# One queue order over all rounds for attention and routed experts, with every pad row scattered instead of pre-filled

## The chip, the cores and the metric

One of the cores of one Trainium2 chip runs the kernel. The metric is the device time of one execution in microseconds (us): median, lowest and highest of the runs. Next to it stands one profiled execution, from which every row below is taken.

## What is computed

The input is 16 sequences of 512 tokens with 256 features. Each token is normalised, and attention and a mixture of experts (MoE), both fed by the normalised token, are added to it:

```python
xn = layernorm(x)
x = x + attn(xn) + moe(xn)

# attention, per sequence: 16 heads, 16 wide for q and k, 64 wide for v and the gates
q, k, v = l2norm(q), l2norm(k), l2norm(v)
sim  = einsum('bhid,bhjd->bhij', q, k)
aggr = einsum('bhij,bhjd->bhid', square(relu(sim)), v)
attn = (tanh(|aggr|) * aggr/|aggr| * tanh(silu(gates))) @ Wout

# MoE: 16 experts of width 128, 4 for each token, from the 2 best of 4 groups, and 2 shared experts
scores = sigmoid(xn @ router.T)
tidx, tw = top4 of the experts in the best two groups; tw = 2.5 * tw / sum(tw)
moe = sum_k tw[k] * down_e(silu(gate_e(xn)) * up_e(xn)) + shared(xn)
```

## The kernel before

**Set-up.** For two sequences at a time SP (the queue that only issues DMAs) loads tokens into `xs`, DVE normalises them (`layernorm`), TensorE turns them, ACT writes the high fp16 half of the turned tokens and POOL the low one (both in `xhl`), and SP stores rows (`xn_d`) and turned tokens (`xt_d`) to HBM. `xhl` has two buffers, so ACT waits for a store to land before it writes again. ACT and DVE also split the weights into two fp16 halves (`high_parts`, `low_parts`). After each pair of sequences SP issues one `fill_slots`: it writes copies of a pad row over an eighth of `slot_d`, the table of 144 blocks of 256 token rows, by expert, through which the routed experts get their tokens. Then `route()` on DVE works out for each token and choice its slot (`slot_no`) and weight (`slot_w`), and the expert of each block (`blk_w`).

**Sixteen rounds**, one sequence each, follow. A round has four stages:

- *head*: the value projections (`V`, 8 of them), the q/k norms on DVE, their fp16 split on ACT and POOL (`split_lo_qk`, 8 operations on POOL), the turns `T` into `qt` and `kt`
- *S*: 32 steps; each has two score products `S` on TensorE, a relu on ACT, a square on DVE and four value products `AV` (two steps behind)
- *tail*: head norms and their chain of small DVE operations, the turn `WT` of the scales
- *O*: 8 output products `O`; each waits for `a_lo`, a subtraction on POOL. The gates `G`, `WB` and the next round's `QK` stand between them. Then DVE takes the two results out (`finish`), and POOL adds them to the output with an accumulating DMA, here called the base add. Its count is `base_added`.

The shared experts take four units in each round, each an up part (`SG`), a high part on ACT and a low part on POOL (`HH`, `hidden_lo`), and a down part (`SD`).

**Rounds 0 to 3** also send the token rows: `send_rows` (`RW`, 16 in each round, in S at every second step) waits for a row tile from SP, copies weight and token number beside the rows, and issues four indirect DMAs to `slot_d`. There are two tile buffers (`xrow`).

**Rounds 4 to 15** also compute 12 blocks each, all inside S. A block is a chain of six items, one step apart: `XT` (turn, TensorE; the high half on ACT), `XL` (low half, DVE), `GU` (gate and up on TensorE, silu on ACT, product on DVE), `HR` (high part on ACT, low part on POOL), `DN` (down on TensorE, `block_out` on DVE), `SC` (`send_block`: POOL issues two indirect DMAs that add 256 rows to the output; it waits for the previous block's rows to have landed).

Every engine executes its own list in order, and the lists are written out by hand: `plan_steps` says at which step an item stands, `tail` what follows the last step, `pe_order` TensorE's list. Three PSUM banks `wk` go round in the order of that list (`RING`), and an operation that fills one waits until its use three places earlier has been emptied.

## Time and profile before

| | |
|---|---|
| median of 3 runs | 3089.48 us (3085.49 to 3090.55) |
| the profiled execution | 3091.26 us, of which the span is 3089.5 us |
| busy shares of the span | TensorE 73%, DVE 59%, ACT 50%, POOL 46% |
| granted TensorE clock, mean | 0.931 |

How to read the rows of the next sections: a row of stretches gives the stretch, its length, then busy us and count of instructions of PE (TensorE), PEld (its weight loads), DVE, ACT and POOL, the granted clock as a share of full speed, the DMA engines' busy share and GB/s. A row of waits says which engine and line waited for which, us in total, times, and the longest. A row of the chain that ended last has start, us, and what ran (a name that begins with DMA is a transfer landing). A row of the order of time has start, us, engine, line, operation, and in brackets idle time before it and what ended it. A grouped row has busy us and mean ns, then the idle time before the group.

### The profile page before, as it was taken

What the parts mean: (1) busy time and instruction counts of PE and PEld (TensorE: products, weight loads), DVE (VectorE), ACT (ScalarE), POOL (GpSimd) and SP (SyncE); (2) the same over time, 40 slices, a digit from 0 to 9 for tenths busy, and PEclk for the clock granted to TensorE, in tenths of its full rate; (3) what the DMA queues carried; (4) which work ended last, traced back from release to release, by engine and by line L of the source; (5) the groups of instructions that cost most, each with busy time, mean ns of one, the idle gap of its engine ahead of it and who ended that gap; (6) DMA issues with size and microseconds to landing.
All of it is one profiled execution on the core that took longest, in us unless ns stands there. A gap on an engine that the chain in (4) does not pass through costs nothing.

```text
span 3089.5 us, 41253 instructions
## 1 busy us (share of the span) xinstructions
PE 2243.1 (73%) x13476; PEld 1210.7 (39%) x13476; DVE 1831.9 (59%) x2961; ACT 1535.4 (50%) x2396; POOL 1423.7 (46%) x1339
## 2 busy tenths in 40 slices
PE   4433758484838887877878787878788787878877
PEld 3322233232314444444434444444444444444443
DVE  6678537272726555565656556565656656565654
ACT  2313536262625555555555555554555455555554
POOL 1211747566663534444353544435354444435343
PEclk9999979697978999999999999999999999999999
DMA  9992433333341413223141322213032222314132
GB/s 354 327 338 95 146 88 117 110 94 118 89 154 18 66 28 49 46 34 53 26 64 21 57 40 37 47 32 64 15 62 35 45 45 31 59 19 66 21 50 40
DMA packets 161519, 247.27 MB, mean 80 GB/s; under 512 B 14945, under 2 KB 147041, under 8 KB 159361
## 3 DMA queue, kind: packets, MB, share of 16 engines
q1 hardware_dynamic: 99104, 164.63, 17.0%
q0 software_dynamic: 62208, 79.99, 15.8%
q8 instruction: 117, 1.92, 0.2%
q14 instruction: 90, 0.73, 0.1%
HBM read 147.84 MB, written 144.25 MB: 95 GB/s over the span
## 4 chain that ended last, share of the span: by engine, by line
PE 37%; issue 21%; POOL 12%; DVE 12%; DMA 11%; ACT 5%; SPq 0%; ACTq 0%; DVEq 0%; POOLq 0%
PE wk L1175 14%; PE av L1259 7%; POOL slot_d L1101 6%; PE acc L1175 6%; DMA out_t<-ye,xg 3%; DMA xt_d<-xhl 2%; PE sim L1244 2%; DMA xrow<-xn_d 2%; PE wk L1306 2%; PE wk L1226 2%; POOL out_t L1083 2%; ACT ring L941 2%; DMA xg<-slot_d 2%; DMA slot_d<-xrow,slot_no 2%; POOL hle L1074 2%
## 5 line engine op out<-in xcount | busy, mean ns | idle before, releaser
L656 DVE TENSOR_TENSOR pr<-ring 128x1024 f32<-128x1024 f32 x512 | 627.6, 1227 | 448.5 <-ACT ring L941 438.2
L941 ACT ACTIVATE ring<-sim 128x1024 f32<-128x1024 f32 x512 | 524.0, 1023 | 291.4 <-PE sim L1244 269.4
L1259 PE MATMUL av<-pr,v 128*64 128x512 f32 x2048 | 550.8, 618 | 20.6 <-ACT wide L975 19.2
L1083 POOL DMA_INDIRECT out_t<-ye,xg x288 | 466.1, 1618 | 69.1 <-issue 69.1
L1074 POOL TENSOR_TENSOR hle<-hfe,hhe 128x256 f16<-128x256 f32 x208 | 244.4, 1176 | 438.6 <-ACT hhe L952 434.0
L1101 POOL DMA_INDIRECT slot_d<-xrow,slot_no x256 | 294.8, 1152 | 76.3 <-issue 59.0
L706 DVE TENSOR_TENSOR gate_sb<-gate_sb,wk 128x512 f32<-128x512 f32 x128 | 87.7, 686 | 345.9 <-PE wk L1334 345.9
L1130 POOL TENSOR_TENSOR pr<-wide,pr 128x512 f16<-128x512 f32 x128 | 162.4, 1273 | 269.2 <-ACT pr L987 269.2
L1069 POOL TENSOR_TENSOR gate_sb<-ring,gate_sb 128x512 f16<-128x512 f32 x128 | 164.1, 1306 | 243.4 <-ACT gate_sb L927 243.4
L947 ACT ACTIVATE sge<-wk,inv_m 128x256 f32<-128x256 f32 x208 | 99.0, 476 | 290.4 <-PE wk L1175 290.4
L1175 PE MATMUL wk<-wa_h,xhl 128*128 128x512 f16 x768 | 199.1, 382 | 57.2 <-DVE blk_w L596 44.4
L663 DVE SCALAR_TENSOR_TENSOR hfe<-wk,up_scale,sge 128x256 f32<-128x256 f32 x208 | 100.3, 482 | 231.9 <-ACT sge L947 223.0
L1244 PE MATMUL sim<-qt,kt 64*128 64x512 f16 x1024 | 205.1, 397 | 36.2 <-issue 18.6
L1244 PEld LDWEIGHTS sim<-qt,kt 64*128 64x128 f16 x1024 | 49.7, 93 | 434.6 <-ACT ring L941 228.9
L1089 POOL TENSOR_TENSOR mark<-pair_sel 1x1 f32<-1x1 f32 x160 | 29.3, 183 | 387.9 <-DVE ye L676 324.3
L1175 PE MATMUL wk<-down_h,hhe 128*128 x288 | 80.4, 279 | 169.1 <-issue 168.6
L1175 PE MATMUL acc<-wo_h,pr 128*128 128x256 f16 x1024 | 177.0, 275 | 30.5 <-POOL pr L1130 30.5
L885 ACT ACTIVATE sq<-wk 128x512 f32<-128x512 f32 x192 | 114.4, 596 | 149.2 <-PE wk L1175 149.2
L1175 PE MATMUL acc<-down_h,hhe 128*128 128x256 f16 x128 | 41.8, 326 | 198.2 <-POOL hle L1074 198.2
L1226 PE MATMUL wk<-id,gate_sb 128*128 128x128 f16 x1024 | 90.9, 265 | 102.8 <-DVE hfe L663 102.8
L1175 PE MATMUL wk<-xhl,wa_h 128*128 128x512 f16 x512 | 162.6, 401 | 2.4 <-ACT gate_sb L980 2.4
L980 ACT ACTIVATE gate_sb<-wk,inv_a 128x512 f32<-128x512 f32 x128 | 87.7, 685 | 153.6 <-PE wk L1175 153.6
(222 smaller groups left out, 4643.4 us busy)
## 6 DMA issues: line engine op xcount, KB each, us to landing
xg<-slot_d SPq DMA_DIRECT2D x147, 258.0 KB
slot_d<-pad_rows SPq DMA_DIRECT2D x8, 4644.0 KB, 19.3
xrow<-xn_d SPq DMA_DIRECT2D x64, 512.0 KB
xs<-x SPq DMA_DIRECT2D x16, 512.0 KB, 5.1
xn_d<-xs SPq DMA_DIRECT2D x16, 512.0 KB, 19.0
xt_d<-xhl SPq DMA_DIRECT2D x16, 512.0 KB, 16.5
xhl<-xt_d SPq DMA_DIRECT2D x16, 512.0 KB, 3.4
out_t<-pr POOLq DMA_DIRECT2D x16, 512.0 KB, 5.9
```

The lines of the kernel that those rows point to most:

```text
L656: tt(pr[:, n:n + 2, :], ring[:, q:q + 2, :], ring[:, q:q + 2, :], ALU.mult).then_inc(square_done, 1)
L885: a(sq[:, n % 2, :], bank(r, key)[:, :], ACT.Square).then_inc(rawsq_done, 1)
L941: a(ring[:, q:q + 2, :], sim[:, :, :], ACT.Relu).then_inc(relu_done, 1)
L1069: tt(lo, src, hi, ALU.subtract).then_inc(qk_lo, 1)
L1074: tt(hle[:, i % 2, :], hfe[:, i % 2, :], hhe[:, i % 2, :], ALU.subtract).then_inc(h_lo, 1)
L1083: pool.indirect_dma_start(out=out, out_offset=bass.IndirectOffsetOnAxis(xg[:, n % XG, j, D + 1:D + 2].bitcast(U32), 0), in_=ye[:, n % 2, j ...
L1101: pool.indirect_dma_start(out=slot_d, out_offset=bass.IndirectOffsetOnAxis(slot_no[:, k, c:c + 1], 0), in_=xrow[:, k % 2, c, :], in_offset ...
L1130: tt(al[:, t % 2, :], agg[:, t, :], ah[:, t % 2, :], ALU.subtract).then_inc(a_lo, 1)
L1175: ins = mm(dst, w[k], xx[k], start=start and i == 0, stop=stop and i == n - 1, skip_group_check=not (start and stop))
L1226: ins = turn(bank16(r, ("T", n))[:, m * P:(m + 1) * P], src[:, m * P:(m + 1) * P], id16[:, :])
L1244: ins = mm(sim[:, half, :], kt[rows, pair, j * P:(j + 1) * P], qt[rows, pair, :], start=True, stop=True)
L1259: ins = mm(av[64 * half:64 * half + 64, :], v32[:, j, h * DV:(h + 1) * DV], pr[:, (2 * s + half) % NH_, :], start=(j == 0), stop=(j == NB ...
```

## The change

The two hand-made lists per kind of round become one plan over all 16 rounds. `TICKS` cuts a round into 59 places with assumed lengths (8 `h`, 4 `t`, 32 `s`, 6 `e`, 9 `o`; 141.8 us in sum). Sixteen chains, 12 blocks and 4 shared units, start at equal distances over the round, head, tail and O included, and a chain may run over into the next round. Row tiles (`RW`) and pad tiles (`PD`) are spread over all places of rounds 0 to 3. Within a place the items stand in the order XL, SC, DN/SD, HR/HH, GU/SG, XT; those of the last place, `('o', 8)`, stand behind `finish` on DVE and behind the base add on POOL. `slot_d` is no longer filled: `route()` works out the numbers of the 4096 slots without a token (`pad_no`), and 32 indirect DMAs on POOL put pad rows there. Weight and token number come to `xrow` by a second DMA from `slot_m` and no longer by two POOL copies. `xg` has five buffers in place of three, the `mark` operations ahead of DMAs are gone, six small loads are reordered, and DVE takes `gated(t + 1)` a place earlier.

```diff
-XG = 3
+XG = 5
+EXP0 = 4
+BLOCKS = [0] * EXP0 + [12] * 12
+TICKS = ([(("h", n), 1.9) for n in range(2 * NB)] + [(("t", n), 2.6) for n in range(NB)]
+         + [(("s", n), 2.3) for n in range(STEPS)] + [(("e", n), 2.6) for n in range(6)]
+         + [(("o", n), 3.0) for n in range(NP_ + 1)])
+UP_CHAIN = (("XT", 0.0), ("XL", 2.0), ("GU", 4.2), ("HR", 7.5), ("DN", 11.0), ("SC", 13.0))
+SHARED_CHAIN = (("SG", 4.2), ("HH", 7.5), ("SD", 11.0))
...
+def plan_round_starts(b):
+    blocks = BLOCKS[b]
+    n = max(blocks + SH, 16)
+    at = [m * n // 16 for m in (1, 4, 7, 10)]
+    length = ROUND_TIME if b < B - 1 else ROUND_TIME - 14.0
...
+    for m in range(n):
+        when = b * ROUND_TIME + 0.5 + m * length / n
...
+    units = [("RW", k) for k in range(TILES)]
+    for k in range(PAD_TILES):
+        units.insert(3 * k + 2, ("PD", k))
+    places = [(b, tick) for b in range(EXP0) for tick, _ in TICKS if b < EXP0 - 1 or tick[0] != "o"]
+    for n, unit in enumerate(units):
+        plan[places[n * len(places) // len(units)]].append(unit)
...
-            def fill_slots(g):
-                n = NBLK * BLK // (B // LNG)
-                sp.dma_start(slot_d[g * n:(g + 1) * n, :].rearrange("(a r) c -> a (r c)", a=16),
-                             pad_rows.rearrange("r c -> (r c)").unsqueeze(0).to_broadcast(
-                                 [16, PADS * ROW])).then_inc(slots_set, 16)
...
+                    sp.dma_start(xrow[:, tau % 2, :, D:D + 2], slot_m[:, tau, :, :]).then_inc(rows_loaded[tau % 2], 16)
...
             def body(r):
-                for k in range(NB):
-                    split_lo_qk(r, k)
-                item(r, ("HH", 0))
-                item(r, ("HH", 1))
+                for n in range(4):
+                    items(r, "h", n)
+                split_lo_qk(r, 0)
+                items(r, "h", 4)
+                split_lo_qk(r, 1)
+                for n in range(5, 8):
+                    items(r, "h", n)
+                split_lo_qk(r, 2)
+                items(r, "t", 0)
+                split_lo_qk(r, 3)
...
                 for t in range(NP_):
                     pool.wait_ge(a_hi, r.n(NP_, t + 1))
                     pool.wait_ge(out_mm, r.n(NP_, t - 1))
                     tt(al[:, t % 2, :], agg[:, t, :], ah[:, t % 2, :], ALU.subtract).then_inc(a_lo, 1)
+                    items(r, "o", t)
                 pool.wait_ge(y_done, r.n(2, 2))
...
+                bases[0] += 1
+                items(r, "o", NP_)
```

`send_block` in its new form, on POOL; `bases[0]` counts the base adds issued so far:

```python
def send_block(g):
    pool.wait_ge(ye_done, g + 1)
    pool.wait_ge(sent, 32 * g)
    pool.wait_ge(base_added, 16 * bases[0])
    for j in range(HALVES):
        pool.indirect_dma_start(...)     # 128 rows each, added to out
```

## Rows read from the trace of the kernel before

**Rows 1.** Stretches of the set-up: to the end of the tokens, and `route()`.

```profile
66.40:191.00 124.60, 60.32 (x266) 55.27 (x265) 77.84 (x201) 41.06 (x52) 27.31 (x14) 1.00 0.97 337
191.00:269.80 78.80, 1.89 (x4) 0.43 (x4) 76.23 (x138) 0.00 (x0) 0.18 (x1) 1.00 0.75 251
```

**Rows 2.** Waits in the first 205 us.

```profile
ACT xhl L866 <- DMA xt_d<-xhl: 27.2, 9, 6.9
...
DVE stats L482 <- DMA xs<-x: 9.1, 2, 6.6
```

**Rows 3.** Stretches of round 2: head, S, tail, O.

```profile
614.40:644.40 30.00, 21.39 (x148) 13.01 (x147) 25.80 (x52) 19.99 (x37) 12.70 (x12) 0.88 0.13 18
644.40:697.90 53.50, 49.71 (x240) 16.19 (x241) 40.30 (x40) 38.77 (x45) 44.84 (x46) 0.97 0.39 129
697.90:758.80 60.90, 16.92 (x95) 8.91 (x95) 10.52 (x28) 10.04 (x18) 39.95 (x55) 0.66 0.45 147
758.80:781.70 22.90, 22.89 (x142) 13.72 (x143) 10.45 (x15) 11.92 (x20) 8.44 (x7) 0.93 0.21 70
```

**Rows 4.** Waits of round 2.

```profile
PE acc L1175 <- POOL hle L1074: 42.0, 1, 42.0
```

**Rows 5.** Stretches of round 7: head, S, tail, O.

```profile
1484.70:1514.70 30.00, 21.40 (x148) 12.97 (x147) 25.80 (x52) 20.03 (x37) 12.71 (x12) 0.88 0.13 18
1514.70:1618.30 103.60, 82.11 (x496) 41.18 (x494) 60.08 (x75) 54.89 (x82) 52.37 (x46) 0.97 0.35 54
1618.30:1640.70 22.40, 17.83 (x101) 9.10 (x101) 10.76 (x28) 9.03 (x18) 6.39 (x8) 0.92 0.20 36
1640.70:1662.00 21.30, 21.25 (x142) 13.38 (x143) 10.49 (x15) 11.96 (x20) 8.48 (x7) 1.00 0.08 26
```

**Rows 6.** The page's DMA issues: KB each, us from issue to landing.

```profile
slot_d<-pad_rows SPq DMA_DIRECT2D x8, 4644.0 KB, 19.3
...
out_t<-pr POOLq DMA_DIRECT2D x16, 512.0 KB, 5.9
out_t<-ye,xg POOLq DMA_INDIRECT x288, 3.8
```

**Rows 7.** POOL's row sends in round 0, grouped: beside S, then after it.

```profile
L1101 POOL DMA_INDIRECT slot_d<-xrow,slot_no x30 | 40.5, 1349 | 9.0 <-issue 6.7 <-POOL xrow L1097 2.3
...
L1101 POOL DMA_INDIRECT slot_d<-xrow,slot_no x35 | 34.4, 982 | 10.4 <-issue 8.5 <-POOL xrow L1097 1.9
```

**Rows 8.** The chain that ended last, tail of round 2.

```profile
719.26 3.10 DMA slot_d<-xrow,slot_no
722.38 4.19 DMA xrow<-xn_d
```

**Rows 9.** The chain that ended last, S of round 7: GU, XT, DN.

```profile
1562.44 1.50 PE wk L1175 x12
...
1564.08 0.63 PE wk L1306 x4
...
1592.79 0.82 PE wk L1175 x6
```

**Rows 10.** TensorE's down products in round 7, grouped.

```profile
L1175 PE MATMUL wk<-down_h,hhe 128*128 x24 | 6.6, 276 | 14.1 <-issue 14.0
```

**Rows 11.** POOL in order of time, S of round 7: HR, then one SC.

```profile
1567.49 1.40 POOL L1074 TENSOR_TENSOR hle<-hfe,hhe 128x256 f16<-128x256 f32 x1 [1.57 <-ACT hhe L952]
...
1571.77 1.57 POOL L1083 DMA_INDIRECT out_t<-ye,xg  x1 [0.17 <-issue]
1573.64 1.54 POOL L1083 DMA_INDIRECT out_t<-ye,xg  x1 [0.31 <-issue]
```

**Rows 12.** POOL in order of time, from round 3 to round 4.

```profile
953.14 1.30 POOL L1135 DMA_DIRECT2D out_t<-pr  x1
961.95 5.72 POOL L1069 TENSOR_TENSOR gate_sb<-ring,gate_sb 128x512 f16<-128x512 f32 x4 [7.50 <-ACT gate_sb L927]
```

**Rows 13.** The base adds by line: ns min/median/max, first and last start.

```profile
L1135 POOL DMA_DIRECT2D out_t<-pr x16: 1275/1283/1375, 446.3 to 3082.2; - x16
```

More of the change, by code:

```diff
@@ L82, in tail @@
-def tail(late):
-    return ([("AV", STEPS - 2), ("G", 0), ("SG", 2), ("N", NP_ - 2), ("AV", STEPS - 1)] + late
-            + [("HH", 2), ("SG", 3), ("N", NP_ - 1), ("G", 1), ("HH", 3), ("SD", 2), ("TH", 0), ("SD", 3),
-               ("WT", 0), ("G", 2), ("WB", 0), ("WB", 1)])
-PLAN, LATE, TAIL = {}, {}, {}
-for _kind in "AB":
-    PLAN[_kind], LATE[_kind] = plan_steps(_kind)
-    TAIL[_kind] = tail(LATE[_kind])
-def pe_order(kind):
+EXP0 = 4
+BLOCKS = [0] * EXP0 + [12] * 12
+assert len(BLOCKS) == B and sum(BLOCKS) == NBLK
@@ new lines @@
+TICKS = ([(("h", n), 1.9) for n in range(2 * NB)] + [(("t", n), 2.6) for n in range(NB)]
+         + [(("s", n), 2.3) for n in range(STEPS)] + [(("e", n), 2.6) for n in range(6)]
+         + [(("o", n), 3.0) for n in range(NP_ + 1)])
+ROUND_TIME = sum(d for _, d in TICKS)
+UP_CHAIN = (("XT", 0.0), ("XL", 2.0), ("GU", 4.2), ("HR", 7.5), ("DN", 11.0), ("SC", 13.0))
[3 more added lines that the diff above has]
+    n = max(blocks + SH, 16)
+    first = sum(BLOCKS[:b])
+    at = [m * n // 16 for m in (1, 4, 7, 10)]
+    length = ROUND_TIME if b < B - 1 else ROUND_TIME - 14.0
+    chains, g, q = [], first, 0
+    for m in range(n):
+        when = b * ROUND_TIME + 0.5 + m * length / n
+        if m in at:
+            chains.append((when, "shared", (b, q)))
+            q += 1
+        elif blocks:
+            chains.append((when, "block", g))
+            g += 1
+    assert q == SH and g == first + blocks
+    return chains
@@ new lines, in tick_at, with plan_all @@
+def tick_at(when):
+    b = min(int(when // ROUND_TIME), B - 1)
+    left = when - b * ROUND_TIME
+    for n, (_, length) in enumerate(TICKS):
+        if left < length:
+            return b * len(TICKS) + n
+        left -= length
+    return B * len(TICKS) - 1
+def plan_all():
+    plan = {(b, tick): [] for b in range(B) for tick, _ in TICKS}
+    for b in range(B):
+        for when, what, key in plan_round_starts(b):
+            n = -1
+            for kind, later in (UP_CHAIN if what == "block" else SHARED_CHAIN):
+                n = min(max(tick_at(when + later), n + 1), B * len(TICKS) - 1)
+                plan[(n // len(TICKS), TICKS[n % len(TICKS)][0])].append((kind, key))
+    stage = {"XL": 0, "SC": 1, "DN": 2, "SD": 2, "HR": 3, "HH": 3, "GU": 4, "SG": 4, "XT": 5}
+    for items in plan.values():
+        items.sort(key=lambda item: stage[item[0]])
+    units = [("RW", k) for k in range(TILES)]
[4 more added lines that the diff above has]
+        plan[places[n * len(places) // len(units)]].append(unit)
+    for b in range(B):
+        for t in range(NP_ - 2):
+            plan[(b, ("s", NB * (t + 1) + LAG + 1))].append(("N", (b, t)))
+    return plan
@@ L407, in _ @@
             sp.wait_ge(route_done, 1)
+            for n in range(2):
+                sp.dma_start(pad_row[:, n, :], pad_rows[n * P:(n + 1) * P, :]).then_inc(pads_loaded, 16)
             tau = 0
@@ L821, in body @@
                     norms_round(link_v, "v")
-                item(r, ("SG", 1))
+                items(r, "t", 1)
                 turned_q(r, 2)
@@ L1052, in body @@
                         raw(r, t - (NP_ - 2), ahead=1)
+                    items(r, "o", t)
+                items(r, "o", NP_)
             loops(act, body)
```

595 lines of the change are left out of this document (296 added, 299 removed).

## The prediction

> **What bounds the kernel now.** I read the stretches by stage first. In the set-up the DMA engines are 0.97 busy up to 191 us while DVE works 77.8 of 124.6 us; then `route()` is a pure DVE chain, 76.2 of 78.8 us [rows 1]. Part of DVE's idle time traces back to DMA: ACT waits 27.2 us in nine goes for stores of `xt_d`, DVE 9.1 us for tokens [rows 2].
>
> In a round without blocks the tail is the odd stage: 60.9 us, in which TensorE works 16.9 and POOL 40.0 [rows 3]. The waits say why: a shared down part waits once for 42.0 us for its low half on POOL [rows 4], since 16 row sends stand ahead of it in POOL's queue. In a round with blocks the tail is 22.4 us, and S, where all 12 blocks are, takes 103.6 us with TensorE busy 82.1; O is TensorE from end to end, 21.25 of 21.3 us [rows 5]. The round takes 177.3 us. The base adds give the frame [rows 12, 13]: set-up to 269.8 us, four rounds to 953.1 (683.3), twelve rounds to 3082.2 (2129.1, 177.4 each), 7.3 to the end of the span, and 1.8 outside it: 3091.3, against a median of 3089.5.
>
> **Set-up: fills out, pad numbers in.** Eight fills of 4644 KB, 38 MB, leave the queue [rows 6]. That is much of what the DMA engines carry up to 191 us, but DVE needs its busy time anyhow, and some of its waits are for ACT and POOL. I give back the 9.1 us of token waits to two thirds (6) and of ACT's 27.2 us for stores about 19, since ACT is ahead of DVE's weight pieces and of the last scores: 25 us off; bounds 10 and 36.3 (all of both rows). `route()` gets six small operations and a copy, the largest half as wide as those that fill its 76.2 us; about 3 us. Set-up: 269.8 - 25 + 3 = 248.
>
> **Rounds 0 to 3: row sends spread.** A send was four issues at 1.35 us beside S and 0.98 after it [rows 7]; with the gaps of 0.3 us between issues (9.0 us over 30) that is 6.3 and 4.8 us; the two POOL copies ahead of it go. I counted the new places from the plan: 8 sends stand in S, the others in head, tail and O, with 8 pads of one issue in each round. POOL's work per round: 8 x 6.3 + 8 x 4.8 + 8 x 1.4 = 100 us, and with the splits, `hidden_lo` and `a_lo` (12.7 + 0.9 + 8.4 busy in [rows 3] beside the sends) 122. The row tiles have two buffers: load 4.2, four issues, landing 3.1 [rows 8] make some 12.5 us for two, so 6.3 each, 100 in a round: not the bound when spread. A round without the stall is 30 + 53.5 + 22.4 (the tail of [rows 5]) + 21.3 = 127.2. POOL is close to full in that, and its sends now stand ahead of things that others wait for: about one send (5) ahead of the splits in the head, the third shared unit late by what POOL's 8 sends, pads and low parts exceed S (60 against 53.5, so 5 of it on the path), one to two sends ahead of `a_lo` at the end of the tail (7), and 3 in O. That gives 35 + 58.5 + 29.4 + 24.3 = 147.2; bounds 127 and 165 (all of the surplus late, as now). Four of them and the 7.3 us by which the first head is longer: 596, for 683.3.
>
> The small DMA for weight and token number goes out beside each tile: 512 pieces of 8 bytes. No row has such a transfer. Below, it is hidden beside the tile (the tile's 4.2 us is also 512 pieces); above, it comes after it in the same time, 8.4 in place of 4.2, and a tile takes 8.4 us in place of 6.3. I take 6.5, nearer to hidden. The Trainium skill (DMA: Bandwidth & Descriptors, Specifications) says that below 512 B the engines do a read-modify-write and lose the line rate, which speaks for the upper figure; by it the sum would be some 40 us longer, as the fourth rival works out from rows.
>
> **Rounds 4 to 15: S.** A steady round now starts 6 blocks in S, 2 in head, 1 in tail, 3 in O, and in S three shared up parts. A block is 1.50 + 0.63 + 0.82 = 2.95 us of TensorE [rows 9] (2.6 where products follow one another). S loses six blocks, 6 x 2.8 = 16.8, and gains 4.5: 82.1 - 16.8 + 4.5 = 69.8 us busy. Idle there was 21.5, of which 14 stood ahead of the down products [rows 10], as `DN` came one step after `HR` with POOL's 1.4 us and an `SC` between [rows 11]. Now it is mostly two steps. So S takes 75 (bounds 70, no idle, and 81, the old idle per block): 28.6 us less.
>
> **O and tail.** O was TensorE all through, so three blocks add 3 x 2.7 = 8. `DN` of `('o', 7)` with its result on DVE now stands ahead of the q/k sums and `finish`: +3. `SC` on POOL, 3.4 us [rows 11], stands ahead of an `a_lo` twice, about 1 us each: 34. The tail's shared units are replaced by about as much of blocks: 22.5.
>
> **Head: the new wait.** `items(r, "o", NP_)` follows the base add on POOL, and in it is the `SC` of the round's eleventh block, which waits for that base add to land. From the base add's issue: 1.3 us issue and 5.9 landing [rows 6, 12], so it goes at 7.2 and ends at 10.6. Behind it stands `HR` of the twelfth, 12.0, and TensorE, which would be at `('h', 1)` after about 3 us, waits there for that low half. The next `SC` (`h2`) must wait until the former has landed, 10.6 + 3.8 = 14.4, and ends at 17.8. Only then comes split 0, which before started at 8.8 [rows 12]: 9.0 later. Among the splits stand one more `SC` and `HR`, of which I count 3 on the path. The head is thus 30 + 12 = 42. The granted clock is 0.88 over the head now [rows 5], so 7.2 of its 30 us are at the lower of the two levels (1.2 GHz), after the engine has waited for the turns' input; that is up to 3.6 us of work. A second wait of 8 us can bring as much again; between 0 and 3.6 I take 1.5: 43.5. Round 4 has no such predecessors: 33 for its head, with two blocks in it.
>
> Round: 43.5 + 75 + 22.5 + 34 = 175, for 177.4. Round 4: 165. The last one has more in S and tail but no next `QK`: 173. Together 165 + 10 x 175 + 173 = 2088, for 2129.1.
>
> **Sum.** 248 + 596 + 2088 + 7.3 + 1.8 = 2941 us. 0.2% is 6 us, about what a measurement here can tell from no change.
>
> **Rivals.**
>
> *The base add's wait costs little* (30%). For it: TensorE has 8.6 us idle in the head [rows 5], which the new wait may only move, if the splits are not what the turns wait for. Then the head is 33, S may reach its floor of 70, and a round 33 + 72 + 22.5 + 32 = 159.5: eleven rounds by 15 less, 2941 - 165 = 2776. Against it: POOL's list is in order, and the wait is explicit.
>
> *Row sends still stall rounds 0 to 3* (12%). For it: POOL would be busy 122 of 147 us, and one late low half stops TensorE. Each round at its upper bound, 165: 4 x 18 = 72 more, 3013.
>
> *Every POOL item of head, tail and O lies on the path, and the kernel gets slower* (7%). Six `SC` and six `HR` a round leave S or sit beside it: 6 x 3.4 + 6 x 1.4 = 29 us; I have counted some 14 of it. With the other 15 a round is 190, and the whole 2941 + 165 = 3106. It decides from a round of 188.7 on: 150 us below the old time are to be used up, 13.7 in each of eleven rounds above 175.
>
> *The 8-byte pieces double the tile's load* (6%). A tile then takes 8.4 us, 16 of them 134, in a round with uneven places some 157: 4 x 10 = 40 more, 2981. The rule named above is what would make it so.
>
> My forecast has 45%. Faster: 45 + 30 + 12 + 6 = 93, of which I put 2 at no change, since the second and fourth rival together leave only some 38 us: faster 91%, same 2%, slower 7%. The forecast's own range is 2880 to 3010; with the first rival below and half of the others above it is 2770 to 3060.
>
> **What would show it.** Right: no `slot_d<-pad_rows` from SP, `route()` starting near 166; no 40 us wait on `hle` in rounds 0 to 3 and those at 140 to 155; S near 75 with six blocks; in each head from round 5 a TensorE wait of 7 to 9 us on POOL's `hle` ahead of a down product, POOL idle some 6 us after the base add's issue, and the first split at 17 to 18 us after it instead of 8.8. Wrong: a head of 33 (first rival), a tail or O far above 22 and 34 (third), POOL waiting for `xrow` over several us a tile (fourth), or a set-up still near 270, which would mean that DVE and not the DMA queue set it.

## The result, and the profile after

The changed kernel takes 3059.31 us (median of 4, 3050.23 to 3073.25), the kernel before beside it 3088.39 us (median of 4, 3085.49 to 3090.55). The ratio is 0.9911, 95% interval 0.9892 to 0.9931: 0.9% or 29 us faster. The forecast was 2941 us, 150 faster. The sign is right and the size is a fifth of what was forecast. The time lies outside the forecast's own range (2880 to 3010) and under 1 us inside the wide one (2770 to 3060). The executions that were profiled took 3073.25 and, before, 3091.3 us. The first is the longest of its four, 14 us above their median, so the stages below add up to 132 us over the forecast where the medians differ by 118. Of the four executions of `e9_e5_e8` below, one took 3853.03 us at a granted clock of 0.58; its ratio is that of the other three (2924.74 to 2933.24 us), and the 2929.45 in its table is the median of all four.

Cut into stages as in the prediction (the head from `finish` of the round before to the first relu, S from the start of the first relu to that of the last, the tail to the first output product, O to the end of `finish`), in us, mean over the rounds:

| stage | before | forecast | after |
|---|---|---|---|
| set-up with `route()` | 270.0 | 248 | 263.8 |
| rounds 0 to 3, sum | 682.9 | 596 | 605.0 |
| a round of 5 to 14: head | 29.2 | 43.5 | 42.7 |
| S | 103.4 | 75 | 81.9 |
| tail | 22.8 | 22.5 | 23.8 |
| O | 22.0 | 34 | 34.4 |
| that round | 177.4 | 175 | 182.9 |
| rounds 4 to 15, sum | 2129.1 | 2088 | 2194.0 |

So 84 us were gained up to round 3, and 65 given back in the twelve rounds after. The stretches of a round in the trace after (length, then busy time and instructions of TensorE, its weight loads, VectorE, ScalarE, GpSimd; the granted clock, the DMA engines' busy share, GB/s): head, S, tail and O of round 11.

```profile
2148.00:2190.80 42.80, 28.13 (x186) 17.57 (x183) 27.60 (x52) 22.52 (x42) 22.55 (x18) 0.84 0.35 62
2190.80:2273.00 82.20, 68.78 (x397) 30.38 (x397) 53.17 (x64) 48.58 (x69) 31.95 (x21) 0.98 0.23 36
2273.00:2297.20 24.20, 17.94 (x98) 9.09 (x95) 12.07 (x30) 9.68 (x19) 6.38 (x6) 0.86 0.19 34
2297.20:2331.60 34.40, 30.31 (x212) 20.06 (x213) 15.65 (x23) 14.40 (x27) 15.89 (x13) 1.00 0.20 32
```

Against [rows 5]: TensorE's busy time in S fell from 82.11 to 68.78 us, as forecast (69.8). But S holds 13.4 us in which it stands, where 5.2 was forecast. The granted clock in S is no lower. TensorE's two largest waits in S, round 7 before and round 11 after:

```profile
PE wk L1175 <- issue: 12.7, 10, 1.6
PE wk L1175 <- DVE xel L670: 5.1, 5, 1.6
```

```profile
PE wk L1232 <- DVE xel L705: 7.7, 5, 4.0
PE wk L1232 <- issue: 2.4, 3, 0.9
```

"issue" here is mostly a down product that waits for its low half: 12.7 us became 2.4. The wait for `xel`, the fp16 tail of a block's tokens that VectorE makes, rose. In the head TensorE stands for 14.7 us, before 8.6, at a granted clock of 0.84, before 0.88.

The set-up and round 2 (head, S, tail, O), in the same columns:

```profile
66.40:181.80 115.40, 59.90 (x264) 54.95 (x263) 75.83 (x201) 41.95 (x52) 24.20 (x13) 1.00 0.41 138
181.80:263.80 82.00, 1.89 (x4) 0.43 (x4) 79.23 (x146) 0.00 (x0) 0.00 (x0) 1.00 0.38 125
576.70:608.30 31.60, 20.51 (x138) 11.71 (x135) 26.58 (x47) 19.31 (x35) 26.31 (x24) 0.87 0.45 115
608.30:677.30 69.00, 56.74 (x276) 19.69 (x278) 41.89 (x45) 40.94 (x51) 48.87 (x43) 0.89 0.52 154
677.30:697.50 20.20, 15.49 (x65) 6.05 (x65) 8.99 (x25) 8.55 (x15) 13.39 (x13) 0.78 0.42 125
697.50:728.20 30.70, 27.06 (x145) 15.63 (x146) 13.87 (x16) 12.01 (x21) 17.08 (x16) 0.81 0.30 91
```

Against [rows 1] the DMA engines' share in the set-up fell from 0.97 to 0.41, and the stretch shortened by 9 us only; VectorE is at work for 75.8 us of it, 77.8 before. Against [rows 3] the tail fell from 60.9 to 20.2 us, and S grew by 15.5.

The head of round 11 on GpSimd, in order of time (start, length, what; in brackets the idle time ahead and what ended it), up to the second send and then the first split:

```profile
2148.28 1.36 POOL L1191 DMA_DIRECT2D out_t<-pr  x1 [5.79 <-DVE pr L752]
2154.95 1.65 POOL L1136 DMA_INDIRECT out_t<-ye,xg  x1 [5.30 <-DMA out_t<-pr]
2156.89 1.57 POOL L1136 DMA_INDIRECT out_t<-ye,xg  x1 [0.30 <-issue]
2157.90 1.27 POOL L1129 TENSOR_TENSOR hle<-hfe,hhe 128x256 f16<-128x256 f32 x1
...
2161.90 1.77 POOL L1136 DMA_INDIRECT out_t<-ye,xg  x1 [2.72 <-DVE ye L711]
...
2167.69 2.36 POOL L1124 TENSOR_TENSOR gate_sb<-ring,gate_sb 128x512 f16<-128x512 f32 x2 [2.15 <-ACT gate_sb L977]
```

and TensorE's waits of over 2 us in the same head:

```profile
2159.38 0.39 PE L1232 MATMUL wk<-down_h,hhe 128*128 x1 [6.04 <-issue]
...
2180.31 0.37 PE L1232 MATMUL acc<-down_h,hhe 128*128 128x256 f16 x1 [3.17 <-issue]
...
2186.23 1.10 PE L1283 MATMUL wk<-id,gate_sb 128*128 128x128 f16 x16 [2.16 <-DVE xel L705]
```

The wait for the base add is there as the prediction told it: the send goes 6.7 us after the add's issue (forecast 7.2), the low half 9.6 (10.6), the first split 19.4 (17 to 18). The down product waits 6.0 us for it (7 to 9).

TensorE's waits from 1000 to 2800 us, some ten rounds, grouped (us in total, times, longest), before and after:

```profile
PE wk L1175 <- issue: 143.4, 115, 1.7
PE wk L1226 <- DVE hfe L663: 63.7, 10, 6.4
PE wk L1175 <- DVE xel L670: 53.3, 51, 2.3
```

```profile
PE wk L1232 <- issue: 100.7, 49, 6.7
PE wk L1232 <- DVE xel L705: 76.2, 54, 4.0
```

The 14 us a round of "issue" became 10, of which 7.5 stand in the head (round 11), 6.0 of them behind the base add. The waits for `xel` rose from 5.3 to 7.6 us a round, though half of the blocks had left S. In S of round 11 one is of 4.0 us, at the first up product, and four are of 0.8 to 1.0: the steps with the other four up products take 3.6 to 3.9 us, where 2.3 to 2.9 are common. The prediction has no word on it. And the wait of 6.4 us in each head for `hfe` is gone, which the prediction doesn't mention either.

### The profile page after: what moved, and what is told of

The parts are those of the page before. It is cut to its first block, busy times and chain, and to the rows that moved or that the text cites. A ratio compares the mean times of both kernels' runs of the same rounds, so it can differ in the third digit from the quotient of the medians.

```text
span 3071.4 us, 41012 instructions
## 1 busy us (share of the span) xinstructions
PE 2296.8 (75%) x13476; PEld 1218.2 (40%) x13476; DVE 1848.7 (60%) x2968; ACT 1528.8 (50%) x2396; POOL 1367.9 (45%) x1083
## 3 DMA queue, kind: packets, MB, share of 16 engines
q0 software_dynamic: 63744, 84.22, 16.3%
## 4 chain that ended last, share of the span: by engine, by line
issue 41%; POOL 25%; PE 18%; DVE 7%; DMA 5%; ACT 2%; POOLq 0%; SPq 0%; ACTq 0%; DVEq 0%
PE wk L1232 10%; POOL out_t L1136 9%; POOL slot_d L1143 5%; POOL hle L1129 4%; POOL pr L1186 4%; DMA out_t<-ye,xg 4%; PE acc L1232 2%; POOL gate_sb L1124 2%; PE av L1316 2%; PE wk L1256 1%; PE sim L1301 1%; DMA xrow<-slot_m 1%; ACT ring L991 1%; DVE big L776 1%; DMA xt_d<-xhl 1%
## 5 line engine op out<-in xcount | busy, mean ns | idle before, releaser
L1136 POOL DMA_INDIRECT out_t<-ye,xg x288 | 478.9, 1663 | 517.1 <-DVE ye L711 410.8
L1316 PE MATMUL av<-pr,v 128*64 128x512 f32 x2048 | 569.5, 637 | 31.1 <-ACT wide L1026 28.3
L1129 POOL TENSOR_TENSOR hle<-hfe,hhe 128x256 f16<-128x256 f32 x208 | 229.3, 1102 | 662.7 <-ACT hhe L1002 656.8
L1143 POOL DMA_INDIRECT slot_d<-xrow,slot_no x256 | 279.4, 1091 | 174.4 <-DMA xrow<-slot_m 99.3
L711 DVE SCALAR_TENSOR_TENSOR ye<-wk,out_scale,xg 128x512 f32<-128x512 f32 x144 | 107.4, 746 | 143.7 <-PE wk L1232 143.6
L1038 ACT ACTIVATE pr<-wide 128x512 f16<-128x512 f32 x128 | 80.4, 628 | 192.1 <-DVE wide L746 174.7
L1124 POOL TENSOR_TENSOR gate_sb<-ring,gate_sb 128x512 f16<-128x512 f32 x128 | 147.8, 1175 | 44.2 <-ACT gate_sb L977 41.6
L1316 PEld LDWEIGHTS av<-pr,v 128*64 128x64 f32 x2048 | 107.7, 139 | 134.1 <-issue 119.2
L1232 PEld LDWEIGHTS acc<-wo_h,pr 128*128 128x128 f16 x1024 | 92.4, 100 | 131.3 <-POOL pr L1186 101.0
L1232 PE MATMUL acc<-wo_l,pr 128*128 128x256 f16 x512 | 143.1, 279 | 0.0
```

What stands on the lines that cost most here:

```text
L711: v.scalar_tensor_tensor(out=ye[:, g % 2, :, :], in0=bank(("DN", g))[:, :].rearrange("p (j d) -> p j d", j=HALVES), scalar=out_scale[:, 0: ...
L1124: tt(lo, src, hi, ALU.subtract).then_inc(qk_lo, 1)
L1129: tt(hle[:, i % 2, :], hfe[:, i % 2, :], hhe[:, i % 2, :], ALU.subtract).then_inc(h_lo, 1)
L1136: pool.indirect_dma_start(out=out, out_offset=bass.IndirectOffsetOnAxis(xg[:, g % XG, j, D + 1:D + 2].bitcast(U32), 0), in_=ye[:, g % 2, j ...
L1143: pool.indirect_dma_start(out=slot_d, out_offset=bass.IndirectOffsetOnAxis(slot_no[:, k, c:c + 1], 0), in_=xrow[:, k % 2, c, :], in_offset ...
L1232: ins = mm(dst, w[k], xx[k], start=start and i == 0, stop=stop and i == n - 1, skip_group_check=not (start and stop))
```

## The experiments

Each kernel was timed beside the kernel before on the same chip (medians there 3075.8 to 3083.9 us). On those chips the changed kernel's ratio of 0.9911 stands for about 3054 us. "The changed kernel" is the base of every diff. The expectations name rival theories, A and B.

### Does the base add's wait cost the head its 13 us?

`e1_scratch`: the attention result is added to a table of its own, so that a send waits for nothing there; the output then lacks that part.

```diff
-                pool.wait_ge(base_added, 16 * bases[0])
...
-                pool.dma_start(out[r.b * T:(r.b + 1) * T, :].rearrange("(k p) d -> p k d", p=P),
+                pool.dma_start(base_d[r.b * T:(r.b + 1) * T, :].rearrange("(k p) d -> p k d", p=P),
```

> The changed kernel, with the base add going to a scratch table in HBM instead of the output (the attention result is left out of the output), so that no SC waits for it; nothing else moves. Theory A (the wait behind the base add is what makes the head 42.6 us): the SC behind the base add goes at once, HR and the down product with it, the 6 us wait of TensorE in the head goes, head 33 to 35 us, in all 11 rounds x 8 = 90 us less than 3059, about 2970. Theory B (the head is long because two blocks and the SCs among the splits are work there, the wait only moves): head 40 or more, less than 25 us in all.

Measured: 3036.92 us, ratio 0.9857 (0.9841 to 0.9874), some 17 us below the changed kernel. A round of 5 to 14 takes 180.9, its head 42.1: theory B (40 or more, less than 25 us in all). GpSimd and TensorE in a head of this run:

```profile
2116.25 1.36 POOL L1192 DMA_DIRECT2D base_d<-pr  x1 [5.79 <-DVE pr L754]
2117.92 1.65 POOL L1137 DMA_INDIRECT out_t<-ye,xg  x1 [0.30 <-issue]
...
2134.46 2.37 POOL L1126 TENSOR_TENSOR gate_sb<-ring,gate_sb 128x512 f16<-128x512 f32 x2 [3.96 <-ACT gate_sb L979]
```

```profile
2125.97 1.89 PE L1233 MATMUL wk<-wa_h,xhl 128*128 128x512 f16 x4 [2.80 <-DVE xel L707]
...
2153.01 1.86 PE L1284 MATMUL wk<-id,gate_sb 128*128 128x128 f16 x16 [2.83 <-DVE xel L707]
```

The wait of 6 us is gone, and the head lost 0.6. The first split comes 18.2 us after the add's issue, and in its bracket waits for ScalarE, not for GpSimd's own queue. What holds this head is VectorE, as far as these rows tell: blocks' `xel` stand in its order behind the chain of the q/k norms, and value products and turns wait for PSUM buffers that those `xel` have to empty. So the prediction's head was right in size and wrong in mechanism: the wait is real and hardly on the path.

### Where should the twelve blocks be?

`e2_in_s` keeps the planner and lets block chains start only in S; `e5_no_head` lets them start anywhere but in the head; `e6_old_blocks` puts them by the list of the kernel before.

```diff
+    times = [(b * ROUND_TIME + 0.5 + m * length / n, "shared") for m in at]
+    times += [(b * ROUND_TIME + 25.7 + m * 61.0 / blocks, "block") for m in range(blocks)]   # e2_in_s
+    times += [(b * ROUND_TIME + 25.7 + m * 106.1 / blocks, "block") for m in range(blocks)]  # e5_no_head
```

```diff
+        if b >= EXP0:                      # e6_old_blocks
...
+            for n in range(BLOCKS[b]):
+                a = n * (STEPS - 5) // (BLOCKS[b] - 1)
+                for d, (kind, _) in enumerate(UP_CHAIN):
+                    plan[(b, ("s", a + d) if a + d < STEPS else ("e", 1))].append((kind, sum(BLOCKS[:b]) + n))
+            continue
```

> The changed kernel, with the twelve block chains of a round started only in S (between 25.7 and 86.7 us of the plan's round), the shared units where they are now. Theory A (the spreading of blocks over head and O is what costs, since S gave back less than head and O took): S 103, head 31, O 22 to 23, a round near 177 as before the change, in all 2194 - 2130 = 65 us less than the changed kernel, 2990 to 3000. Theory B (the plan as such, its order inside a place and its five buffers, costs the time, not where the blocks stand): a round stays at 182 or more, 3055 or more.

> The changed kernel, with the twelve block chains of a round started evenly from the first step of S to the middle of O (25.7 to 123 us of the plan's round), none in the head, the shared units where they are now. Theory A (a block costs 3.6 to 4.3 us in S, tail and O, but about 7 in the head, where its turn holds a PSUM bank through DVE's norm chains and its SC stands between POOL's splits): head 27 to 29, S 92 with 9 blocks, tail 24, O 28 to 31, a round 173 to 176, in all about 85 us below the changed kernel, 2965 to 2985. Theory B (a block costs the same 4 us wherever it stands): a round 180 or more, 3035 or more.

> The changed kernel, with blocks and shared units of rounds 4 to 15 at the places that the kernel before gave them (blocks in S at its steps, shared units in head and tail); set-up, rounds 0 to 3, buffers and code as in the changed kernel. Theory A (the placing of the blocks is all of what rounds 4 to 15 lost; everything else of the change is neutral there): a round 177 again, 2194 - 2130 = 64 less than the changed kernel, about 2990. Theory B (the order inside a place, the mark operations, the order of gated or five buffers matter as well): a round differs from 177.4 by over 2 us.

| kernel | time, us | ratio (95%) | head | S | tail | O | round |
|---|---|---|---|---|---|---|---|
| changed | 3054 | 0.9911 (0.9892 to 0.9931) | 42.7 | 81.9 | 23.8 | 34.4 | 182.9 |
| e2_in_s | 3066.40 | 0.9957 (0.9939 to 0.9976) | 26.4 | 113.6 | 19.5 | 22.0 | 181.5 |
| e5_no_head | 2944.31 | 0.9549 (0.9523 to 0.9575) | 26.4 | 89.2 | 25.3 | 31.8 | 172.7 |
| e6_old_blocks | 2937.68 | 0.9538 (0.9511 to 0.9564) | 26.6 | 101.8 | 22.2 | 22.0 | 172.7 |

With the old list a round is 172.7 us: 10.2 below the changed kernel, 122 us in twelve rounds, and 4.7 below the kernel before. So the new places are what made rounds 4 to 15 longer, and the rest of the change made them shorter. Where those 4.7 come from, TensorE's waits in the same stretch of this run show, beside the list of before above:

```profile
PE wk L1242 <- issue: 143.7, 121, 1.6
PE wk L1242 <- DVE xel L715: 30.2, 31, 1.6
PE wk L1293 <- DVE qt L689: 29.1, 11, 2.7
```

The waits for low halves are those of before (143.7 against 143.4). The one of 6.4 us a round for `hfe` is not there: the rewritten loops on VectorE make a shared part's `hfe` ahead of the last steps of the value norms, before it stood behind them. In its place is one of 2.6 for `qt`, and the head is 26.6 us for 29.2. That edit was in the diff, and I costed it at nothing. The other 2.1 us are 1.6 in S, where the waits for `xel` fell from 5.3 to 3.0 us a round, and 0.6 in the tail; which part of the rewritten loops gives them was not tested. All of this is read from rows, no run has the one edit alone.

That `e5_no_head` and `e6_old_blocks` come out alike says that an even spacing over S, tail and O is worth as much as the dense list in S; it is the blocks in the head that cost. They add 16.3 us there (42.7 against 26.4) and take 7.3 from S. Both came out faster than their theory A (2965 to 2985, and about 2990): for `e6_old_blocks` that surprise is the 4.7, which is theory B's sign. Packing twelve chains of the planner into S (`e2_in_s`) brought steps of up to 10 us; head and O fell as in theory A, but S took 113.6 us for its 103, and the time is theory B's.

### Which orders on VectorE cost S its 7 us?

`e3_v_first` puts VectorE's six value scalings ahead of its part of the last head tick; `e8_xl_first` puts `xel` ahead of a step's square product; `e16_e3_e8` has both, at the change's own places.

```diff
                 turned_q(r, 3)
-                items(r, "t", 3)
                 for n in range(2, 2 * NB):
                     unit_v(r, n)
+                items(r, "t", 3)          # e3_v_first
```

```diff
+                    for kind, n in PLAN[(r.b, ("s", s))]:
+                        if kind == "XL":
+                            block_lo(n)   # e8_xl_first
                     square(r, s)
-                    items(r, "s", s)
+                    items(r, "s", s, skip="XL")
```

> The changed kernel, with DVE's last six value scalings put ahead of the items of place t3. Theory A (S is longer than the 75 us forecast since the scalings, held back by the product of the block in t3, delay the first squares and the low half of the next block; TensorE waits 4.0 us for it at step 2): steps 1 and 2 shrink from 4.05 + 6.0 to about 5 us, S 78, 12 x 4 = 48 us less, about 3010. Theory B (the block's own product is then late by the same 4.2 us and TensorE waits for that): S unchanged within 1 us, 3050 to 3060.

> The changed kernel, with DVE's low half of a block (XL) ahead of the square of the same step, no longer behind it. Theory A (each GU in S waits about 0.9 us for a low half that stands behind a square): GU steps from 3.6 to 3.9 down to 2.7 to 2.9 us, S 5 us less a round, 12 x 5 = 60 us less than the changed kernel, about 2995. Theory B (the square is then late and the value products wait in its place): S within 1 us of 82.

> The changed kernel with the two orders on VectorE that were each faster alone, and the blocks where the change puts them: the six value scalings ahead of its part of the last head tick (S 81.9 to 78.6 us), and xel ahead of the square product (S 81.9 to 76.3). Theory A (the 82 us of S where 75 was forecast are TensorE's waits for xel, of two kinds: behind the long first steps and behind the square products): S 73 to 75 us, so that the forecast's term of 75 holds; head, tail and O stay at 42.7, 25, 34.4, the round 176 to 177, the time 3054 - 19 - 51 = 2985 us (2970 to 3000). Theory B (the same waits were counted in both, as in the kernels without a block in the head, where the second order gave nothing on top): S 76 to 77, 3000 to 3010 us.

| kernel | time, us | ratio (95%) | head | S | tail | O | round |
|---|---|---|---|---|---|---|---|
| e3_v_first | 3040.45 | 0.9860 (0.9844 to 0.9877) | 42.9 | 78.6 | 25.3 | 34.7 | 181.5 |
| e8_xl_first | 3005.35 | 0.9745 (0.9712 to 0.9778) | 42.9 | 76.3 | 24.2 | 34.4 | 177.9 |
| e16_e3_e8 | 2964.48 | 0.9613 (0.9592 to 0.9633) | 42.4 | 74.9 | 23.6 | 34.4 | 175.3 |

This settles the failed term. With both orders S is 74.9 us where 75 was forecast, and the round 175.3 where 175 was. Theory A held for S in all three; the times were 2964.48 for its 2970 to 3000 with both, 3005 for its 2995 with `xel` first, and 3040 for its 3010 with the scalings first, since the tail gave 1.5 us of 3.3 back and the third step still took 4.3 us. TensorE's waits for `xel` ahead of up products from 1000 to 2800 us are 76.2 us in the changed kernel; in `e3_v_first`, `e8_xl_first` and `e16_e3_e8` they are

```profile
PE wk L1232 <- DVE xel L705: 42.4, 56, 1.0
```

```profile
PE wk L1237 <- DVE xel L705: 27.8, 14, 2.9
```

```profile
PE wk L1237 <- DVE xel L705: 1.6, 9, 0.2
```

S of round 11 with both is 75.5 us with TensorE at work 69.27, so that 6.2 are left for all waits:

```profile
2120.70:2196.20 75.50, 69.27 (x390) 30.35 (x390) 49.33 (x59) 47.63 (x67) 29.34 (x21) 0.95 0.25 38
```

The two waits have one cause in two places. An `xel` that stands behind a square product of 1.2 us is ready 0.8 to 1.0 us after TensorE wants it, in four steps of a round. In the first steps of S the one behind the six value scalings is 4 us late:

```profile
2197.20 0.68 DVE L705 TENSOR_TENSOR xel<-wk,xeh 128x512 f16<-128x512 f32 x1
...
2198.01 0.67 PE L1232 MATMUL wk<-xeh,gate_h 128*128 128x256 f16 x2 [4.02 <-DVE xel L705]
```

The gain together (7.0 us of S) is less than the sum of the two (8.9).

### A later up product

`e4_gu_late` answers the same wait from the other side: `GU` and all behind it one step later in every chain.

```diff
-UP_CHAIN = (("XT", 0.0), ("XL", 2.0), ("GU", 4.2), ("HR", 7.5), ("DN", 11.0), ("SC", 13.0))
-SHARED_CHAIN = (("SG", 4.2), ("HH", 7.5), ("SD", 11.0))
+UP_CHAIN = (("XT", 0.0), ("XL", 2.0), ("GU", 6.5), ("HR", 9.8), ("DN", 13.3), ("SC", 15.3))
+SHARED_CHAIN = (("SG", 6.5), ("HH", 9.8), ("SD", 13.3))
```

> The changed kernel, with GU and all that follows it one place (2.3 us of the plan) later in each chain, block and shared. Theory A (each GU waits about 0.9 us for its low half, since DVE squares first, in the place between them): the waits of TensorE on xel in S, 7.7 us a round, go, 5 to 8 us less a round, about 2980. Theory B (TensorE's order is tied to the relu loop anyway, and each item costs its full time on top of 1.69 us per step): GU steps stay above 3.0 us, a round loses less than 2 us, 3035 to 3060.

Measured: 3109.31 us, ratio 1.0093 (1.0072 to 1.0114), slower than the kernel before, and outside both theories; the round 186.4, head 42.6, S 80.5, tail 27.1, O 36.1. TensorE's row for `xel` is gone from the list, and others have grown (1000 to 2800 us):

```profile
PE acc L1232 <- issue: 61.0, 10, 6.2
PE wk L1232 <- POOL hle L1129: 49.9, 10, 5.7
...
PE av L1290 <- DVE wst L735: 30.9, 9, 3.5
```

The first two stand in the head, whose length is that of the changed kernel all the same: the second is the wait behind the base add (6.2 us in round 10 of the changed kernel, 4.8 here), the first was of 3.2 us there and is of 6.2 here. The third stands in the tail and was 17.6 us in all; tail and O together took 5.0 us more. In S a step with an up product still takes 3.5 to 3.9 us, as theory B said, and down products wait 8.0 us in S of round 10, so that of 7.7 us of waits for `xel` S gave back 1.4. To shift a whole chain moves each of its stages onto new neighbours.

### Do the fills cost the set-up anything?

`e7_fills`: eight fills of 4128 KB again, to a table that nobody reads, and a wait for them at the end of the set-up.

```diff
+                sp.dma_start(fill_d[g * 16 * BLK:(g + 1) * 16 * BLK, :].rearrange("(a r) c -> a (r c)", a=16),
+                             pad_rows.rearrange("r c -> (r c)").unsqueeze(0).to_broadcast([16, BLK * ROW])).then_inc(slots_set, 16)
```

> The changed kernel, with eight fills of 4128 KB sent again by SP at their old places, to a table that nothing reads, and waited for by POOL at the end of the set-up. Theory A (the set-up is a chain of DVE, ACT and POOL; the fills cost only what ACT and DVE waited for their DMAs): route starts 8 to 11 us later, at 190 to 193, 10 us more in all. Theory B (DMA bandwidth bounds the set-up, as its 0.97 share suggests, and the removed POOL and ordering changes hid it): 20 us or more.

Measured: 3059.57 us, ratio 0.9931 (0.9908 to 0.9954), beside 0.9911 for the changed kernel: 6 us by the two, whose intervals overlap. Neither theory (10 us, or 20 and more) is borne out. The set-up:

```profile
66.40:185.00 118.60, 59.78 (x264) 54.83 (x262) 79.15 (x200) 41.81 (x52) 24.03 (x13) 1.00 0.95 336
185.00:267.00 82.00, 1.89 (x4) 0.43 (x4) 79.19 (x146) 0.00 (x0) 0.00 (x0) 1.00 0.60 204
```

The DMA engines are 0.95 busy as before, and the set-up ends at 267.1 us, not 263.8: 3.3 us for 33 MB. VectorE is 79 us at work of 118.6. Little of its idle time is a queue's: in the changed kernel without fills VectorE, up to 182 us, waits 12.5, 11.7 and 11.6 us for ScalarE's halves of three weights, and 6.4 for tokens.

### Combinations

`e9_e5_e8` is `e5_no_head` with `xel` first, `e11_e5_e8_e3` has the value scalings first too, `e10_e6_e8` is `e6_old_blocks` with `xel` first.

> Two edits that were each faster alone, together: no block chain starts in the head (2944.31 us alone), and VectorE makes a block's fp16 tail (xel) ahead of the step's square product, not behind it (S 81.9 to 76.3 us for the 7 or so blocks whose tail falls in S, 0.8 us each). Theory A (a round is a sum of places in which TensorE waits, and the two edits shorten different ones): 8 blocks in S, so S 89.2 - 6.4 = 82.8 and the round 172.7 - 6.4 = 166.3, the time 2944 - 12 x 6.4 = 2867 us (2855 to 2885). Theory B (with the head empty of blocks VectorE has slack in S, so its order no longer matters): 2935 to 2945 us.

> The first kernel of this batch with VectorE's six value scalings ahead of its part of the last tick of the head (alone on the changed kernel: S 81.9 to 78.6, tail 23.8 to 25.3, 19 us in all). The long first steps of S (6.3 us for the third) should shrink to 2 to 3 us. Theory A: 2 to 3 us in S, 1 to 1.5 given back in the tail, so 12 to 20 us below the first kernel of the batch. Theory B (without a block in the head the only item of that tick is a shared expert's product, whose hidden values are then late for the down product of step 0): no change or up to 10 us slower than the first kernel.

> The blocks placed as in the kernel before (all twelve in S, each stage one step after the other; 2937.68 us alone), with VectorE's xel ahead of the step's square product. Theory A (0.8 us for each of 12 tails in S): S 101.8 - 9.6 = 92.2, the round 163, the time 2938 - 12 x 9.6 = 2823 us (2800 to 2850). Theory B (with two or three blocks' stages in most steps TensorE's own 82.9 us of work in 101.5 and ScalarE's relu set the steps, and the tail is mostly in time): S 97 to 100, 2880 to 2915 us.

| kernel | time, us | ratio (95%) | head | S | tail | O | round |
|---|---|---|---|---|---|---|---|
| e9_e5_e8 | 2929.45 | 0.9500 (0.9478 to 0.9523) | 26.4 | 89.2 | 24.3 | 31.7 | 171.7 |
| e11_e5_e8_e3 | 2933.35 | 0.9518 (0.9500 to 0.9536) | 26.3 | 89.7 | 24.4 | 31.7 | 172.2 |
| e10_e6_e8 | 2880.14 | 0.9346 (0.9326 to 0.9366) | 26.7 | 96.1 | 23.4 | 22.0 | 168.2 |

`e10_e6_e8` is the fastest kernel here, 6.5% below the kernel before. Its TensorE waits 5.7 us for `xel` from 1000 to 2800 us, where `e6_old_blocks` has 30.2. S fell by 5.7 us a round and the time to the lower end of theory B's 2880 to 2915; the row for `xel` explains some 2.4 of the 5.7, the rest was not traced. In `e11_e5_e8_e3` the scalings' order gave nothing without a block in the head, as its theory B said.

`e9_e5_e8` didn't do what theory A said, nor for the reason of theory B. Its steps with an up product did fall (round 9: two from 4.1 to 2.9 us, one from 5.4 to 4.2, one from 3.4 to 2.9). But one step, the 28th, which took 3.8 us, now takes 4.3 to 8.8, and the one after it 4.2 for 2.7 (round 9), so that S stayed at 89.2. GpSimd and TensorE in it (round 9):

```profile
1806.55 2.60 POOL L1142 DMA_INDIRECT out_t<-ye,xg  x1 [5.03 <-DVE ye L712]
1809.44 2.60 POOL L1142 DMA_INDIRECT out_t<-ye,xg  x1 [0.30 <-issue]
1811.50 2.25 POOL L1135 TENSOR_TENSOR hle<-hfe,hhe 128x256 f16<-128x256 f32 x1
```

```profile
1813.94 0.39 PE L1238 MATMUL wk<-down_h,hhe 128*128 x1 [3.90 <-issue]
...
1816.82 1.97 PE L1322 MATMUL av<-pr,v 128*64 128x512 f32 x4
```

Two issues of 2.60 us, elsewhere 1.56, stand ahead of a split, and the down product waits 3.9 us. From the end of that wait to 1818.8 us the granted clock is 0.50, the lower of TensorE's two levels (1.2 GHz): four value products take 1.97 us, elsewhere 1.08.

### Is it the order on GpSimd?

`e13_sc_late` plans the sends of `e9_e5_e8` 15.6 us behind a block's start, not 13.0. `e14_e10_hr` is `e10_e6_e8` with the split ahead of the sends in a step that has both. `e15_late_hr` has both edits on `e9_e5_e8`.

```diff
-UP_CHAIN = (... ("DN", 11.0), ("SC", 13.0))
+UP_CHAIN = (... ("DN", 11.0), ("SC", 15.6))     # e13_sc_late, e15_late_hr
```

```diff
-    stage = {"XL": 0, "SC": 1, "DN": 2, "SD": 2, "HR": 3, "HH": 3, "GU": 4, "SG": 4, "XT": 5}
+    stage = {"XL": 0, "HR": 1, "HH": 1, "SC": 2, "DN": 2, "SD": 2, "GU": 4, "SG": 4, "XT": 5}   # e14_e10_hr, e15_late_hr
```

> The kernel with no block in the head and xel first (2929.45 us), with each block's two accumulate DMAs planned 15.6 us behind its start instead of 13.0, so one step later on GpSimd. In that kernel's round 9 GpSimd issues them at 1806.55 and 1809.44, for 2.60 us each, and the next block's split of the hidden values starts at 1811.50 behind them; the down product waits 3.9 us for it, and the step takes 8.8 us. Theory A (the order of the accumulate DMAs and the split on GpSimd takes back what xel first gives): that step falls to 2.9 us, the next to 2.5, S to 82 or 83, the round to 165 or 166, 2860 to 2875 us. Theory B (the split is late by its own chain, through ScalarE's fp16 copy, and the DMAs only fill its wait): 2925 to 2935 us. Theory C (the later accumulate DMAs hold back the next load or the next result, two buffers of which there are): over 2935 us.

> The kernel with the blocks placed as in the kernel before and xel first (2880.14 us), with GpSimd's split ahead of the accumulate DMAs in the 7 steps a round that hold both. Theory A (the split behind two issues of 1.63 us is what lengthens those steps, 3.4 to 6.8 us long): 1 to 2 us of each of 7 steps, 84 to 170 us in all times a half that other waits keep, 2790 to 2840 us. Theory B (the DMAs then wait behind a split whose input is not there, and the down products were in time): 2875 to 2900 us.

> The kernel with no block in the head, xel first, and each block's accumulate DMAs planned 15.6 us behind its start (2932.23 us), with GpSimd's split ahead of the accumulate DMAs where a step holds both: in the run before, both came to stand in step 27, the DMAs still first, so that its 8.8 us (two issues of 2.60 us, the split 1809.52 behind them, a down product waiting 3.9 us) stayed. Theory A (the order on GpSimd is what makes that step long): step 27 falls to 2.9 us, step 28 to 2.7, S from 89 to 82 or 83, 2855 to 2875 us. Theory B (as in the run with the blocks placed as before: the DMAs come too close behind one another, GpSimd waits 3 to 5 us for the landing of the pair before and the split stands behind that): 2930 to 3000 us.

| kernel | time, us | ratio (95%) | head | S | tail | O | round |
|---|---|---|---|---|---|---|---|
| e13_sc_late | 2932.23 | 0.9522 (0.9500 to 0.9544) | 26.5 | 89.1 | 24.5 | 31.8 | 171.8 |
| e14_e10_hr | 3161.38 | 1.0258 (1.0232 to 1.0285) | 26.8 | 114.0 | 29.0 | 22.3 | 192.2 |
| e15_late_hr | 3042.29 | 0.9885 (0.9863 to 0.9908) | 26.5 | 90.8 | 25.4 | 38.1 | 180.8 |

`e13_sc_late` tells nothing, though its time is theory B's: the later sends fell into the split's own step, still ahead of it, and the long step stayed. `e15_late_hr` turned them round there, and that step fell in round 9 from 8.8 to 4.5 us. So the order did make it long. But the 21st step now takes 8.5 us for 2.7, where a shared down product waits 3.8 us for its low half, and O grew by 6.4, where an output product waits 4.6 us for GpSimd (both round 9). The time is above both theories. `e14_e10_hr` shows the other price of a late send. GpSimd in its round 9:

```profile
1867.95 1.56 POOL L1151 DMA_INDIRECT out_t<-ye,xg  x1 [0.99 <-issue]
1869.82 1.56 POOL L1151 DMA_INDIRECT out_t<-ye,xg  x1 [0.30 <-issue]
1874.36 2.06 POOL L1151 DMA_INDIRECT out_t<-ye,xg  x1 [2.98 <-issue]
1876.73 1.55 POOL L1151 DMA_INDIRECT out_t<-ye,xg  x1 [0.30 <-issue]
1877.74 1.25 POOL L1144 TENSOR_TENSOR hle<-hfe,hhe 128x256 f16<-128x256 f32 x1
```

A block's sends wait until those of the block before have landed. Pushed behind a split they come so close to their predecessors that GpSimd stands still for 3 us, and the next split stands behind them: TensorE waits 4.8 us for it, and 3.5 to 4.7 in three more steps, which take 6.8 to 12.7 us (in `e10_e6_e8` 4.2 to 5.6). This is outside both theories, and slower than the kernel before. It is the kind of wait that the prediction saw at the base add, now inside S.

## Why the prediction was wrong

**The term that failed: "So S takes 75".** The prediction was right in what leaves S (busy 68.8 us against 69.8) and in what the spacing gives (waits of down products in S down from 12.7 to 2.4 us). It put all idle time of S at 5.2 us, with no term for `xel`; that wait rose instead, from 5.1 to 7.7 us. Its order on VectorE, behind the step's square product, is that of before, and in the later steps four up products now wait 3.6 us, where before, in round 7, three of them waited 3.4 us: so this part did not fall with the number of blocks. Why not, was not tested; with fewer products in a step TensorE may come to the up product sooner. In the first steps the value scalings now go behind an item of the head that they were ahead of, and the wait at the first up product rose from 1.5 to 4.0 us. `e16_e3_e8` shows that this order, in its two places, is the whole of the difference: 74.9 us. 7 us in each of twelve rounds are 84 of the 118 us missed. To see it ahead of the run, one had to go through VectorE's list of a step as I had gone through GpSimd's; the row for `xel`, 53.3 us over ten rounds, stood in the trace of before.

**Set-up, "25 us off": 9 off, and 6 with `route()`, which grew by 3 as forecast.** 16 us too much was taken off. I gave 19 back for ScalarE's waits for stores. They did fall (to 7.9 us in two goes), but VectorE's four largest waits for ScalarE did not: 43.7 us before, 47.2 after. `e7_fills` puts the fills at some 3 us by the traces and 6 by the ratios.

**Rounds 0 to 3: 596, measured 605.0.** The stall went as forecast: the 42 us wait of [rows 4] is not there. The stages are split otherwise: S 68.5, not 58.5, tail 20.5, not 29.4. These two errors cancel, which is luck. A round is 151.3 us where 149 was forecast (147.2, and a quarter of the first head's 7.3). GpSimd's waits for tiles in these rounds are

```profile
POOL slot_d L1143 <- DMA xrow<-slot_m: 99.3, 10, 89.6
```

and the one of 89.6 us stands ahead of the first send, so the other nine come to 9.7 us: the fourth rival's sign is not there. A tile's load took 5.62 us in the chain of round 2, for 4.19 in [rows 8]:

```profile
630.23 3.86 DMA slot_d<-xrow,slot_no
...
634.51 5.62 DMA xrow<-slot_m
```

That is 1.4 us more with the 512 pieces of 8 bytes beside the tile, by this one pair of rows: between hidden and doubled, as was taken. But the send's landing, which has no such pieces, grew as well, from 3.10 us to 3.86. The rule of the Trainium skill (DMA: Bandwidth & Descriptors, Specifications) that was weighed in the prediction would have brought the upper figure; no run here has the small pieces by themselves, so what of the 1.4 us is theirs stays open.

**Head, "12 us on the path" for the base add's wait: 42.7 where 43.5 was forecast, and by another path.** Each event is there, within some 2 us of its forecast time. But `e1_scratch` takes the wait away, and only 0.6 us of the head goes. A count of one queue's delays gave the right length by luck: two queues were late by about the same, and I had looked at one. The clock's 1.5 us can't be told apart: the granted clock of the head is 0.84 after and 0.88 before. The first rival (base add's wait costs little) was right in its premise and wrong in its time, since it gave the head 33 us.

**Tail and O, 22.5 and 34: 23.8 and 34.4.** Right, by their terms.

**The rival on the other side** (every item on the path, from 188.7 us a round) was nearer than its 7%: the round came to 182.9, 5.8 below it, and `e4_gu_late`, with `GU` and what follows one step later in each chain, passed the line of no gain. What kept the whole on this side were rounds 0 to 3, with 78 us, and the set-up, with 6.

**A gain that I costed at nothing:** the head is 2.6 us shorter in `e6_old_blocks`, where TensorE no longer waits 6.4 us for `hfe`. In the changed kernel that wait is gone too, but the blocks in the head make it longer by far more.

Open: why a block in the head holds VectorE's norm chain for as long as it does was read from the chain and from `e1_scratch`, not tested by itself. The value scalings' order was not tried with the blocks placed by the old list.

## What to carry to other kernels

When work is moved between stages, go through the in-order list of each engine that it touches, and ask for each item which stands ahead of it that was not there before. The forecast did that for one engine and missed 84 us on another. Even spacing is no end in itself: the head was a chain of small dependent operations with little to spare on any engine, and blocks there cost 16 us for 7 saved. Before moving work, try the cheap order: two swaps on VectorE gave 3% on the changed kernel, and one of them with the blocks left where they were gave the fastest version, 0.9346.
